# A fused adaLN attention and mixture-of-adapters block on one Trainium2 core: the router moved into attention's last row, row statistics spread over units, Newton rounds on VectorE

## What is computed

```
sa, ca, ga, sb, cb, gb = modulation vectors from silu(c) @ wmod
h  = layernorm(x) * (1 + ca) + sa
x1 = x + ga * (causal_attention(layernorm(h) * gamma + beta) + h)
f  = layernorm(x1) * (1 + cb) + sb
probs = softmax(f @ Wr.T)            # 8 experts, the best 2 picked per row
base: silu(f @ Wg.T) * (f @ Wu.T) @ Wd.T
expert e: silu(gate + lora_e) * (up + lora_e), then its own low-rank down product,
          weighted by its probability (0 where it is not picked)
out = x1 + gb * (base + experts)
```

## Time and profile before

| | |
|---|---|
| runs (3) | 688.88 us median, 688.78 to 689.23 |
| the profiled execution's own time | 688.73 us |
| its span in the profile | 686.9 us |
| PE busy | 652.9 us, 95% of the span |
| DVE busy | 474.2 us, 69% |
| POOL busy | 377.4 us, 55% |
| ACT busy | 356.7 us, 52% |
| clock granted to PE, mean | 0.994 of full speed |

### The profile page before, as it was taken

One profiled execution on the slowest core, in us unless ns is written; L12 is line 12 of the kernel. 1 busy time (PEld: TensorE's weight loads), 2 busy tenths in 40 slices (PEclk: granted clock), 3 DMA queues, 4 the chain that ended last, 5 costly groups with the idle time before them and its releaser, 6 DMA issues.

```text
span 686.9 us, 10710 instructions
## 1 busy us (share of the span) xinstructions
PE 652.9 (95%) x3772; PEld 558.8 (81%) x3772; DVE 474.2 (69%) x1146; ACT 356.7 (52%) x642; POOL 377.4 (55%) x473
## 2 busy tenths in 40 slices
PE   4869999999999999999999999999999999999996
PEld 3559987888879987888878897798888998788885
DVE  5997678478886677658976767747987657637323
ACT  4635455546455546465455446564454546654543
POOL 3785345538577236647576516654765635543644
PEclk9989999999999999999999999999999999999999
DMA  8300020000000020000000001000000000000000
GB/s 311 122 1 1 1 62 0 1 2 31 0 2 31 1 62 0 1 1 32 0 1 32 1 1 62 0 1 18 15 1 1 32 1 1 0 1 1 31 0 32
DMA packets 14054, 15.45 MB, mean 22 GB/s; under 512 B 1328, under 2 KB 12720, under 8 KB 14000
## 3 DMA queue, kind: packets, MB, share of 16 engines
q1 hardware_dynamic: 14000, 14.76, 6.4%
HBM read 10.57 MB, written 4.19 MB: 21 GB/s over the span
## 4 chain that ended last, share of the span: by engine, by line
PE 82%; DVE 12%; issue 2%; POOL 2%; DMA 1%; ACT 1%; DVEq 0%; SPq 0%
PE ps L1263 76%; PE ps L1272 6%; DVE xr L856 2%; DVE hid L1103 1%; DVE rstd L829 1%; DVE zb L844 1%; DMA xs<-in_L_attn_x 1%; DVE xT_lo L890 1%; POOL ring_lo L469 1%; DVE mv L836 1%; DVE tr_full L856 1%; ACT act_s L709 1%; DVE zb L927 0%; DVE stat L841 0%; DVE nr_a L827 0%
## 5 line engine op out<-in xcount | busy, mean ns | idle before, releaser
L469 POOL TENSOR_TENSOR ring_lo<-hid,ring_hi 128x512 fp32r<-128x512 f32 x144 | 189.3, 1319 | 115.9 <-ACT ring_hi L717 115.2
L1103 DVE TENSOR_TENSOR hid<-act_s,ps 128x512 f32<-128x512 f32 x120 | 81.9, 684 | 82.0 <-ACT act_s L709 81.4
L709 ACT ACTIVATE act_s<-ps 128x512 f32<-128x512 f32 x120 | 71.7, 597 | 123.0 <-PE ps L1263 122.4
L717 ACT ACTIVATE ring_hi<-hid 128x512 fp32r<-128x512 f32 (+1 forms) x144 | 90.3, 627 | 16.2 <-DVE hid L1101 8.7
L461 POOL TENSOR_TENSOR xT_lo<-tr_full,xT_hi 128x512 fp32r<-128x512 f32 x28 | 35.9, 1297 | 33.5 <-ACT xT_hi L588 33.5
L1263 PE MATMUL ps<-wdT_hi,ring_hi 128*128 128x256 f32 x192 | 53.6, 285 | 0.0
L1263 PE MATMUL ps<-wdT_lo,ring_hi 128*128 128x256 f32 x192 | 53.2, 282 | 0.0
L1263 PE MATMUL ps<-wdT_hi,ring_lo 128*128 128x256 f32 x160 | 45.2, 282 | 0.0
L1263 PE MATMUL ps<-tm_hi,bgT_hi 128*128 128x512 f32 x96 | 39.5, 411 | 5.7 <-DVE hid L1103 5.7
L1263 PE MATMUL ps<-vv_hi,pT_hi 128*128 128x256 f32 x144 | 43.3, 301 | 0.0
L476 POOL TENSOR_TENSOR xr<-xr,y_gb 128x256 f32<-128x256 f32 x31 | 22.1, 739 | 34.2 <-DVE y_gb L1138 34.2
(11 more groups left out here) (229 smaller groups left out, 2026.4 us busy)
## 6 DMA issues: line engine op xcount, KB each, us to landing
xs<-in_L_attn_x SPq DMA_DIRECT2D x4, 1024.0 KB, 5.6
out<-xr SPq DMA_DIRECT2D x7, 512.0 KB, 3.0
s_mod<-in_L_wmod SPq DMA_DIRECT2D x1, 1024.0 KB, 8.8
s_qkvT<-in_L_attn_qkv SPq DMA_DIRECT2D x1, 768.0 KB, 10.3
s_wg<-in_L_ffn_Wg SPq DMA_DIRECT2D x1, 704.0 KB, 7.4
s_wu<-in_L_ffn_Wu SPq DMA_DIRECT2D x1, 704.0 KB, 8.6
s_wd<-in_L_ffn_Wd SPq DMA_DIRECT2D x1, 640.0 KB, 7.3
s_mod<-in_L_wmod SPq DMA_DIRECT2D x1, 512.0 KB, 6.9
```

What stands on the lines that cost most here:

```text
L469: pool.tensor_sub(ring[1][:, place(n), :], hid[:, n % HID, :], ring[0][:, place(n), :].bitcast(fp32)).then_inc(h_lo.sem, 1)
L709: nc.scalar.activation(act_s[:, n % 2, :], ps[:, 2 * (n % 2), :], ACT.Silu).then_inc(silu_ready.sem, 1)
L717: nc.scalar.activation(ring[0][p0:P, place(n), :], hid[p0:P, n % HID, :], ACT.Copy).then_inc(h_hi.sem, 1)
L1103: V.tensor_mul(hid[:, n % HID, :], act_s[:, n % 2, :], ps[:, 2 * (n % 2) + 1, :]).then_inc(h_ready.sem, 1)
```

## The change

The change moves work and adds no arithmetic on PE.

1. In attention's last scores round (`i == NT - 1`) PE transposes the first half's normalised rows, behind the transposes of tile 6 and ahead of the values of tile 5; DVE scales them ahead of its low part of tile 6, and ACT copies the high parts right behind the exponentials of tile 7. Then PE makes the router's logits ahead of the values of tile 7, the adapters' inputs next, then the values of tile 7, then the first mask, half of the first base product, the second mask, and the rest. DVE forms the last row tile of `x1` behind the router, behind the low parts of the adapter inputs and behind two more row statistics. POOL waits for the values of tile 7 before it writes its first masked product.
2. The second half's row statistics, on DVE as before, are cut into pieces behind units 3 (`x1_stats`), 4 (moments), 5 (guess and one round) and 6 (two rounds and `shift`). The statistics of the next batch's rows move from units 6 and 7 to 7 and 8.
3. The Newton rounds of the next batch's second norm go from POOL to DVE, behind unit 13, and the normalised rows are written behind units 14 to 17, two each, instead of 15 to 17.

```diff
         def body(b, last):                      # POOL
...
                             if r == 0:
+                                pool.wait_ge(pv_ready.sem, pv_ready.at(b, NT - 1))
                                 for m in range(1, 4):
...
-                            if r == 13:
-                                for it in range(NEWTON):
-                                    newton(b, LN1_H, 0, NT, it)
```

```diff
                     scores_exp(i)               # ACT
+                    if i == NT - 1:
+                        for k in range(KT):
+                            tr_high(b, KT * NC + k, xT[0][:, 0, k, :])
...
-                tr_high(b, KT * NC, xT[0][:, 0, 0, :])
                 probs_high(NT - 1)
-                tr_high(b, KT * NC + 1, xT[0][:, 0, 1, :])
...
-                                act.wait_ge(rstd_ready.sem, rstd_ready.at(b, LN2_B))
+                                act.wait_ge(shift_ready.sem, shift_ready.at(b, 0))
```

```diff
-                    if i == NT:                 # DVE, attention
-                        ffn_scale(0, 0)
                     if i >= 1:
                         t = i - 1
                         dve.wait_ge(probs_ready.sem, probs_ready.at(b, t))
                         mark(V.reciprocal(rinv[:, t:t + 1], rowsum[:, t:t + 1]))
+                        if i == NT - 1:
+                            ffn_scale(0, 0)
...
-                    if i >= 2:
+                    if 2 <= i < NT:
                         x1_product(i - 2)
...
+                x1_product(NT - 2)              # DVE, behind attention
                 router_shift(0)
                 x1_stats(TC)
-                x1_stats(TC + 1)
                 router_probs(0)
                 router_top()
                 router_picks()
                 spread_masks(0)
-                x1_product(NT - 1)
-                x1_stats(TC + 2)
                 for g in range(2):
                     adapter_input_low(0, g)
+                x1_stats(TC + 1)
+                x1_stats(TC + 2)
+                x1_product(NT - 1)
                 masked(0, 0)
...
                     hidden(r)                   # DVE, first half
-                    if r == 5:
+                    if r == 3:
                         x1_stats(TC + 3)
+                    if r == 4:
                         moments(range(TC, NT))
                         mark(V.tensor_scalar(neg_mean[:, TC:NT], mv[:, TC:NT, 0], -1.0, None, ALU.mult))
-                        rsqrt(TC, TC)
-                        dve.sem_inc(norm_ready.sem, 1)
-                        V.tensor_mul(shift[:, TC:NT], neg_mean[:, TC:NT], rstd[:, TC:NT]).then_inc(rstd_ready.sem, 1)
+                    if r == 5:
+                        link(guess(TC, TC))
+                        newton(TC, TC, 1)
+                    if r == 6:
+                        newton(TC, TC, NEWTON - 1)
+                        V.tensor_mul(shift[:, TC:NT], neg_mean[:, TC:NT], rstd[:, TC:NT]).then_inc(shift_ready.sem, 1)
...
-                        if r in (6, 7, 11, 12):
-                            i = 2 * (6, 7, 11, 12).index(r)
+                        if r in (7, 8, 11, 12):
+                            i = 2 * (7, 8, 11, 12).index(r)
                             x_stats((i, i + 1))
...
-                            guess(0, NT).then_inc(norm_ready.sem, 1)      # second half, r == 12
-                        if r == 15:
-                            dve.wait_ge(rstd_ready.sem, rstd_ready.at(b, LN1_H))
+                            link(guess(0, NT))
+                        if r == 13:
+                            newton(0, NT, NEWTON)
...
-                        for i in {15: (0, 1, 2), 16: (3, 4, 5), 17: (6, 7)}.get(r, ()):
+                        for i in {14: (0, 1), 15: (2, 3), 16: (4, 5), 17: (6, 7)}.get(r, ()):
                             normalise(i, zb, z_ready, z_tile(i))
```

```diff
-                    else:                       # PE, attention, round 8
-
-                        for k in range(KT):
-                            pe.wait_ge(z2_ready.sem, z2_ready.at(b, TC - 1))
-                            pe.wait_ge(probs_ready.sem, probs_ready.at(b, NT - 2))
-                            transposes(b, KT * NC + k, k, k, [zb[:, tile, :] for tile in range(TC)])
...
+                    if i == NT - 1:
+                        pe.wait_ge(z2_ready.sem, z2_ready.at(b, TC - 1))
+                        for k in range(KT):
+                            transposes(b, KT * NC + k, k, k, [zb[:, tile, :] for tile in range(TC)])
                     if i >= 2:
                         probs_values(i - 2)
...
                 pe.wait_ge(weight_lo, LATE)
-                pe.wait_ge(probs_ready.sem, probs_ready.at(b, NT - 1))
-                probs_values(NT - 1, range(PV_FIRST))
                 logits(0)
-                probs_values(NT - 1, range(PV_FIRST, NT))
+                pe.wait_ge(pt_lo.sem, pt_lo.at(b, NPT - 1))
                 adapter_inputs(0)
+                probs_values(NT - 1)
+                pe.wait_ge(x1_ready.sem, x1_ready.at(b, NT - 2))
+                pe.wait_ge(masks_spread.sem, masks_spread.at(b, 0))
+                mask(0, 0)
                 base(0, 0, 0, (0,))
                 pe.wait_ge(x1_ready.sem, x1_ready.at(b, NT - 1))
-                for m in range(2):
-                    pe.wait_ge(masks_spread.sem, masks_spread.at(b, 0))
-                    mask(0, m)
+                mask(0, 1)
                 base(0, 0, 0, (1,))
```

More of the change, by code:

```diff
@@ L229, in adaln_attention_moe_lora @@
         x1_ready = signal("x1_ready", NT)
-        norm_ready = signal("norm_ready", 4)
-        rstd_ready = signal("rstd_ready", 4)
+        norm_ready = signal("norm_ready", 2)
+        rstd_ready = signal("rstd_ready", 2)
+        shift_ready = signal("shift_ready", 1)
         z2_ready = signal("z2_ready", NT)
@@ L304, in pt_banks @@
             return [(first + q, q * TC, min(TC, i + 1 - q * TC)) for q in range(-(-(i + 1) // TC))]
-        LN2_A, LN2_B, LN1_X, LN1_H = range(4)
+        LN2_A, LN1_X = range(2)
         NEWTON = 3
         T_BANKS = ((4, 5), (0, 1))
-        MASK_BANKS = ((7, 6, 4, 5), (3, 4, 5, 6))
+        MASK_BANKS = ((6, 7, 4, 5), (3, 4, 5, 6))
         LOGIT_BANK = (2, 7)
-        PV_FIRST = TC
         SPLITS = [("wg", s_wg[:, k, :], [w[:, k, 0:F] for w in wgT]) for k in range(KT)]
@@ L502, in _ @@
             setup_steps = steps[1]
-            POOL_STEPS = 3 * (4 * NEWTON - 1) + 1 + NT
+            POOL_STEPS = 2 * (4 * NEWTON - 1) + 1 + NT
             def body(b, last):
@@ L820, in guess, with newton @@
                 return V.tensor_scalar(y.bitcast(i32), nr_i[:, lo:lo + n], -1.0, float(0x5f3759df), ALU.mult, ALU.add)
-            def rsqrt(lo, n):
+            def newton(lo, n, rounds):
                 v, a, y = nr_v[:, lo:lo + n], nr_a[:, lo:lo + n], rstd[:, lo:lo + n]
-                link(guess(lo, n))
-                for _ in range(NEWTON):
+                for _ in range(rounds):
                     link(V.tensor_mul(a, y, y))
@@ L829, in rsqrt @@
                     link(V.scalar_tensor_tensor(y, a, 1.5, y, ALU.add, ALU.mult))
+            def rsqrt(lo, n):
+                link(guess(lo, n))
+                newton(lo, n, NEWTON)
             def moments(tiles):
@@ L977, in _ @@
             setup_steps = steps[1]
-            VSTEPS = 107
+            VSTEPS = 117
             def body(b, last):
```

## The result

| | before | after |
|---|---|---|
| runs, median (us) | 688.94 (688.78 to 689.23, 4 runs) | 694.49 (693.09 to 694.57, 4 runs) |
| ratio to before, 95% interval | | 1.0076, 1.006 to 1.0092 |
| the profiled execution (us) | 688.73 | 694.46 |
| its span (us) | 686.9 | 692.7 |
| clock granted to PE, mean | 0.994 | 0.988 |

The change makes the kernel 5.5 us slower. Forecast were 686.6 us and a range of 682.0 to 689.3. One run of the four, 693.09, is 1.4 us shorter than the profiled one, with a mean granted clock of 0.990 instead of 0.988.

The account below looks back on a forecast made before the run. PE, busy 652.9 of 686.9 us, was taken as the bound, so only its waits could be won. Router 0, row statistics -2.0 + 1.05, Newton rounds -1.2 made -2.1 from 688.73: 686.6 us, range 682.0 to 689.3.

Parts of the forecast that it names:

- The row statistics: Second half's statistics on DVE: wait before unit 8 goes; -2.0 us in the last batch, +0.35 in each other.
- the order at the last gate step: Batches 0 to 2: POOL's low part of unit 9 goes first, 0.15 us ahead; fourth gate step waits some 1.2.
- The pair that the prediction read for this: DVE and POOL at 354.5: POOL asked 0.10 us earlier and went ahead; the DVE row took 1.37 us.
- one new wait right ahead of matmuls of 16 and 8 columns: PE before logits(1) in batches 0 to 2: a new wait of 1.1 us.
- another twelve matmuls before: PE before the base of unit 12 in batches 0 to 2: a new wait of 0.8 us.
- The Newton rounds: Batch boundaries, rounds on DVE: new 0.95 us wait before unit 16, second transposes earlier; -0.4 us per boundary, -1.2 in three.
- with each of the row pairs behind 15, 16 and 17 held once by POOL: Normalised rows on DVE: on this assumption the last row is written at 357.2, second transposes start at 357.25 instead of 357.62.
- The bound, +0.5 per boundary: Bad end for the Newton rounds at each batch boundary: the first row pair is held too; +0.5 instead of -0.4 us.
- The router: Attention's last row: PE does the same matmuls in another order, with no wait to remove; 0 us.
- The bound of +0.5 per batch: Upper bound on the router's cost in attention's last row, taken as 0; the lower bound was -0.2 us.
- No difference: Rival: boundaries at +0.5 us each, one more POOL subtraction in DVE's way behind units 14 to 17; 689.3 us, chance 0.15.
- slower: Rival: late last row tile of x1 makes PE wait up to 1.7 us per batch for second mask; 693.4, chance 0.09.

Follow-up runs that it names:

- e11: e1 with only the fourth gate step moved from behind unit 9 to behind unit 10; median 685.34 us, ratio 0.9953.
- e4: e1 with DVE's four gate steps moved from units 8 and 9 to units 13 and 14; median 681.63 us, ratio 0.9896.
- e1: The kernel before with only the row statistics cut in pieces (part 2 of the change); median 692.08 us, ratio 1.0038.
- e7: e1 with PE's logits(1) put behind the second base product of group 2 instead of between the two; median 692.39 us, ratio 1.0048.
- e2: The kernel before with only part 3: Newton rounds on DVE, normalised rows written two per unit; median 692.08 us, ratio 1.0046.
- e6: e2 with the normalised rows written three, one, three and one behind units 14 to 17; median 688.12 us, ratio 0.9986.
- e8: e4 with Newton rounds on DVE and the rows written three, one, three, one as in e6; median 681.53 us, ratio 0.9894.
- e10: e4, Newton rounds left on POOL, with rows written four, three and one behind units 15 to 17; median 681.06 us, ratio 0.9889.
- e3: The full change with parts 2 and 3 put back, so the router part alone; median 689.71 us, ratio 1.0009.
- e9: e8 with one Newton round behind unit 13, two behind 14, and rows four, three, one behind units 15 to 17; median 680.25 us, ratio 0.9876.

## Why the prediction was wrong, step by step

**The row statistics: right in mechanism, and better than forecast.** The wait before unit 8 went, and in the last batch the gain of 2 us is there (1.8 us from the third boundary's transposes to the end, after 0.16 that the router takes there). In the other batches the order at the last gate step turned as the text said. DVE and POOL of the kernel after, batch 1:

```profile
277.73 0.68 DVE L868 SCALAR_TENSOR_TENSOR gated<-bc 128x512 f32<-128x512 f32 x1
278.93 0.91 DVE L871 TENSOR_SCALAR gated<-gated 128x512 f32<-128x512 f32 x1
279.87 1.72 DVE L874 SCALAR_TENSOR_TENSOR bc<-y_gb,gated 128x512 f32<-128x512 f32 x1
281.51 0.68 DVE L1106 TENSOR_TENSOR hid<-act_s,ps 128x512 f32<-128x512 f32 x1
...
279.75 1.29 POOL L469 TENSOR_TENSOR ring_lo<-hid,ring_hi 128x512 fp32r<-128x512 f32 x1 [0.20 <-ACT ring_hi L716]
```

The fourth gate step, at 279.87, took 1.72 us instead of 0.69: POOL's low part of unit 9 came at 279.75, 2.02 us behind the gate step at 277.73 (2.00 was worked out). Waits of 0.52 and 1.10 us followed before unit 12 and the logits, 1.6 in all where 1.95 were put. The last matmul ahead of unit 8's adapters, at 269.08 before, is now

```profile
272.42 0.40 PE L1271 MATMUL ps<-xT_hi,wuT_lo 128*128 128x512 f32 x1
```

and from there to the logits it is 13.82 us (to 286.24), where it was 13.83 (to 282.91): 0.0 per batch in place of +0.35. Two terms were off by a little. The gates came 1.0 us earlier and not 0.79, and the fourth step was held for 1.03 us and not 1.13. e11, which moves that one step, shows that it is the cause, and e4, which moves all four, agrees. The pair that the prediction read for this had, in the row at 354.61, a VectorE step with one tensor input; a step with two was held in the row at 268.00, and here.

**The term that is missing: the clock of PE.** The prediction counted every wait of PE as time lost once. It took none of them as something that changes the speed of what comes after, though it forecast one new wait right ahead of matmuls of 16 and 8 columns and another twelve matmuls before. The two falls cost 3.0 us of the 5.7; they alone would have turned the forecast gain of 2.1 us into a loss. The profiles of e1, e7 and e11 have falls, those of e2 to e6 and e8 to e10 don't. The page "TensorE: Matmul & The Clock Gate" of the Trainium skill, section "HAM oscillation — how this bites in real kernels", warns of a clock that falls over and over when gaps of PE recur; it has them as gaps far longer than these, and here the measurement decides.

**The Newton rounds: wrong, by one POOL subtraction.** The first half of the step held. One Newton step took 1.22 us, and the product of unit 14 came 3.6 us behind that of unit 13 (3.3 were worked out), so that PE waits 1.06 us before unit 16:

```profile
349.82 0.69 DVE L1104 TENSOR_TENSOR hid<-act_s,ps 64x512 f32<-64x512 f32 x1
...
351.34 1.22 DVE L826 SCALAR_TENSOR_TENSOR nr_a<-nr_a,nr_v 128x8 f32<-128x8 f32 x1
...
353.40 0.69 DVE L1106 TENSOR_TENSOR hid<-act_s,ps 128x512 f32<-128x512 f32 x1
```

The step that failed is "with each of the row pairs behind 15, 16 and 17 held once by POOL". The last pair was held twice, 2.24 us, since by then POOL had two low parts waiting in a row. The second hold alone is worth some 0.95 us per boundary: the second row started at 360.57 and ended with POOL's second subtraction, at 361.92, where such a row takes 0.40. The product of unit 14, 0.3 us later than worked out, is a smaller part of the same error; the rest of it was not followed further. The second transposes came 1.1 us later than before instead of 0.4 earlier, the queries 0.4 later still in one batch: +1.1, +1.5 and +1.1, 3.7 in all, where -1.2 were put (e2: 3.35). This is the largest error of the sum. The bound, +0.5 per boundary, was too narrow; it allowed for one held pair more and not for two subtractions in a row. e6 shows it from the other side: with one row behind unit 17 instead of two, and the others moved forward, the kernel is 4.0 us faster. One row in the last place is not enough by itself, as e10 shows.

**The router: 0 was too low by 0.9 us.** In the change it costs 0.48 us in batch 0 and 0.16 in each other one. The last row tile of x1 came nearly when it was said to, but the sum left out its `settle`: DVE sat 0.15 us between the statistics and the product (last column of the row):

```profile
255.61 0.48 DVE L1001 SCALAR_TENSOR_TENSOR xr<-ps,rinv,xs 128x256 f32<-128x256 f32 x1 [0.15 <-DVE stat L992]
```

The 0.35 us more of batch 0 are a wait of DVE for its own `top` before L1051, 0.50 us at 88.5, where it is 0.15 in batch 1; e3 has it in batch 0 too and, in batch 1, 0.50 instead of 0.15 us ahead of the product. What makes such a wait longer at times is open. The bound of +0.5 per batch just held.

**The sum**, with the sizes measured in the profile after: row statistics 0 - 2.0, boundaries 3.7, router 0.95, clock 3.0: 5.7 us, as between the two profiled executions. Forecast were 1.05 - 2.0, -1.2, 0 and nothing. Of the rivals none had this outcome. "No difference" had the boundaries at +1.5, less than half of what they cost, and "slower" sought the loss at the second mask, where 0.95 of its 6.8 us turned up. So the steps that failed are two: the boundaries with their row pairs "held once by POOL", off by 4.9 us, of which the second hold is some 2.9, and the clock taken as constant, off by 3.0.

**Open.** What decides between a fall and none at equal waits (batch 1 of the kernel after against 0 and 2) is not settled; the runs show only what stood ahead of each fall. Narrow matmuls without a wait beside them were not enough: no profile has a fall behind the logits of a first half, nor behind `logits(1)` in e4, e8, e9 and e10. Whether a wait of this length anywhere in that stretch would do without them was not tried.

## What to carry to other kernels

When a stall is taken out of one engine's path, work out which queue order it had been keeping: a late PE had kept ACT, and so POOL, behind a VectorE step, and a lead of 1.6 us turned that pair round. A string of small VectorE steps with their data in SBUF should be counted with one POOL subtraction in its way, and with two where POOL has a backlog; work that no one awaits (here the gates) belongs behind the step that someone does. A wait of TensorE beside narrow matmuls cost more than its own length here, when the clock of what followed was halved, and runs that spread in steps of 1.4 us or more went with it. A gain measured on a part alone should be looked up wait by wait before it is added to another: e6 and e4 both counted the last batch's wait.

## What the hardware showed that was not expected

The clock of PE fell to 1.2 GHz for 3.4 or 6.8 us behind, or during, the 16 matmuls of 16 and 8 columns that follow a wait of 1.1 us, with PE busy for 6.7 of the 8 us before; each 3.4 us cost 1.5. Behind a wait of 0.41 us it still fell once in the profile of e11, and the clocks of its other runs (0.984 to 0.990) go with more such falls. Waits of 1.2 and 1.4 us between matmuls of 256 and 512 columns did not bring it down. Steps in a kernel's own runs went along with it: 688.6 to 695.1 us in e1, against a spread of 0.3 to 0.9 us in the kernels whose profiles have no fall.
